# Experts' outputs stored by indirect DMA into two dense halves, and one later transfer that fills the empty slots of a mixture of experts

## The reference, cut to what matters

```python
def ffn(x, ...):                       # x: 1024 tokens x 256
    ys = geglu(xf @ Ws1 + bs1) @ Ws2 + bs2            # shared expert
    logits = (xf @ Wr + br) / TAU
    top_val, top_idx = top_k(logits, 2)               # two experts for each token
    top_w = softmax(top_val)
    h = einsum('nd,edh->enh', xf, We1) + be1          # 12 experts, 256 -> 2*768
    yE = einsum('enh,ehd->end', geglu(h), We2) + be2
    return ys + einsum('end,ne->nd', yE, w)           # w holds top_w at top_idx
```

## Time and profile before

| what | value |
|---|---|
| median of 3 runs | 1594.03 us (1591.66 to 1597.79) |
| the profiled execution | 1593.92 us, span 1592.2 us |
| TensorE busy | 1359.0 us, 85% |
| VectorE busy | 1344.2 us, 84% |
| ScalarE busy | 1053.1 us, 66% |
| GpSimd busy | 986.2 us, 62% |
| moved by DMA | 132.87 MB, mean 83 GB/s |
| queue of SP | 94696 packets, 62.99 MB |
| queue of GpSimd | 9312 packets, 67.90 MB |
| stages | start-up to 34, attention to 706, state space to about 1260, experts from 1279 to the end |

### The profile page before, as it was taken

The page is one execution under the profiler, slowest core; times in us unless marked ns, Lnnn a source line. Parts: engine busy times, 40 slices in busy tenths (PEclk is TensorE's granted clock), DMA queues, the critical chain, the costliest instruction groups (busy, mean ns, idle before and its releaser), DMA issues. The chain is left out here.

```text
span 1592.2 us, 33554 instructions
## 1 busy us (share of the span) xinstructions
PE 1359.0 (85%) x12662; PEld 1021.3 (64%) x12662; DVE 1344.2 (84%) x1703; ACT 1053.1 (66%) x2455; POOL 986.2 (62%) x828
## 2 busy tenths in 40 slices
PE   4899999999999999979677667677676899999992
PEld 4688888888888888765233333333333688888881
DVE  3899999999999999987599999999999635666662
ACT  3656666666666666535599899899899234555550
POOL 1778888788888878656166666666666341323323
PEclk9999999999999999999799999999999999999996
DMA  4511111111111111007454110200000016888872
GB/s 120 191 36 43 43 36 46 40 43 43 43 43 36 49 37 30 1 2 153 129 97 63 22 24 1 38 9 1 1 1 1 1 62 267 304 310 310 305 269 86
DMA packets 104155, 132.87 MB, mean 83 GB/s; under 512 B 39514, under 2 KB 95265, under 8 KB 100552
## 3 DMA queue, kind: packets, MB, share of 16 engines
q1 hardware_dynamic: 94696, 62.99, 16.1%
q0 software_dynamic: 9312, 67.90, 12.0%
HBM read 110.44 MB, written 14.45 MB: 78 GB/s over the span
## 5 line engine op out<-in xcount | busy, mean ns | idle before, releaser
L564 POOL TENSOR_TENSOR half<-prob 128x512 f32<-128x512 f32 (+1 forms) x208 | 266.7, 1282 | 108.5 <-ACT prob L600 106.9
L596 ACT ACTIVATE prob<-ps_s,mx 128x64 f32<-128x64 f32 (+1 forms) x624 | 151.5, 322 | 236.3 <-DVE prob L709 236.3
L1359 DVE TENSOR_TENSOR state<-ps_u,state 128x1024 f32<-128x1024 f32 x252 | 296.7, 1219 | 4.3
L704 DVE TENSOR_REDUCE mx<-ps_s 128x16 f32<-128x1024 f32 (+1 forms) x208 | 253.2, 1217 | 14.9 <-PE ps_s L637 11.2
L1318 PE MATMUL ps_y<-state,cz 128*32 128x256 f32 x2048 | 247.5, 384 | 2.1 <-DVE state L1359 1.1
L637 PE MATMUL ps_s<-qbd,kT 64*128 64x256 f32 (+1 forms) x1664 | 217.4, 396 | 23.0 <-ACT prob L596 17.5
L1245 ACT ACTIVATE ps_a<-A,dt 128x256 f32<-128x256 f32 x504 | 210.4, 463 | 35.1 <-DVE state L1354 35.1
L709 DVE TENSOR_TENSOR prob<-ps_s,mx 128x832 f32<-128x832 f32 (+1 forms) x208 | 213.0, 1024 | 7.1
L1229 POOL TENSOR_TENSOR state<-direct,state 128x1024 f32<-128x1024 f32 x64 | 151.6, 2369 | 84.3 <-PE ps_y L1318 84.2
L1300 PE MATMUL ps_u<-x_rows,b_diag 48*128 48x256 bf16 x1024 | 78.1, 272 | 138.2 <-DVE state L1359 134.8
L637 PEld LDWEIGHTS ps_s<-qbd,kT 64*128 64x128 f32 (+1 forms) x1664 | 151.0, 184 | 67.2 <-issue 35.9
(11 more groups left out here) (260 smaller groups left out, 3116.8 us busy)
## 6 DMA issues: line engine op xcount, KB each, us to landing
raw<-in_ctxT_dram SPq DMA_DIRECT2D x80, 268.0 KB, 2.8
x_rows<-ssm_x SPq DMA_DIRECT2D x96, 64.0 KB
raw<-in_ctxT_dram SPq DMA_DIRECT2D x16, 261.0 KB, 2.8
b_diag<-zeros SPq DMA_DIRECT2D x2, 2048.0 KB, 9.0
x_slots<-zeros SPq DMA_DIRECT2D x1, 3456.0 KB, 14.1
xg<-x_slots SPq DMA_DIRECT2D x27, 128.0 KB, 6.5
y_slots<-y SPq DMA_DIRECT2D x27, 128.0 KB, 4.5
ssm_x<-xp SPq DMA_DIRECT2D x6, 384.0 KB, 3.9
```

The costliest lines, as they stand in the source:

```text
L564: pool.tensor_tensor(half[0:rows, :, :], prob[0:rows, g % SLOTS, :, 0:L // 2], prob[0:rows, g % SLOTS, :, L // 2:L], ALU.add).then_inc(hal ...
L704: nc.vector.tensor_reduce(mx[0:rows, g % 2, :], part, AX_X, ALU.max, negate=True)\
L1359: nc.vector.tensor_tensor(h, flat(ps_u[k % 2][:, :, :]), h, ALU.add).then_inc(state_ready, 1)
```

## The change

Five edits belong together.

1. `x_slots` becomes `slot_rows`, a DRAM tensor whose rows have 257 elements: 256 features and a row number. A tile `blank` of 257 columns takes the place of `zeros`; its last column, `unused`, is made by an `iota` and holds 2048 plus the partition. One transfer fills all 3456 rows with it. It is issued behind the chunks of element 3 (CLEAR_AT), and the state-space loads behind those of element 5 (SSM_AT); both stood behind those of element 1.
2. At the head of `experts` GpSimd makes `rows`: for both choices the normalised tokens copied (128x2048 each) with the row number of the token (token, or 1024 + token) in the last column. The 16 scatters store rows of 257 elements.
3. In the routed loop SP no longer stores `y`. It loads for each tile the row numbers (`info`, one element a partition) two tiles ahead, once the put that used the buffer before has landed. GpSimd stores `y` with an indirect transfer (`put_rows`) at those row numbers of `routed`, which is the first 2176 rows of `y_slots`; unused slots go to the rows from 2048 on. The put of tile i-3 stands behind the weight loads of tile i.
4. VectorE's copy of `y` waits for the put that used the buffer, not for the store.
5. After the last put SP loads `back` with eight plain transfers, one for each token tile, of 256 rows each, in place of the 16 indirect gathers.

```diff
+        SSM_AT, CLEAR_AT = 5, 3
...
-                if n == 1:
+                if n == SSM_AT:
                     load_ssm(sp, d, m, ssm_loaded)
-                    sp.dma_start(d["x_slots"].rearrange("(t p) d -> p t d", p=P),
-                                 sb["zeros"][:, :].unsqueeze(1).broadcast_to([P, RTILES, D])).then_inc(slots_cleared, 16)
+                if n == CLEAR_AT:
+                    sp.wait_ge(ones_ready, 1)
+                    sp.dma_start(d["slot_rows"].rearrange("(t p) d -> p t d", p=P),
+                                 sb["blank"][:, :].unsqueeze(1).broadcast_to([P, RTILES, D + 1])).then_inc(slots_cleared, 16)
...
+            c.link(pool.iota(sb["unused"][:, :].bitcast(U32), pattern=[[0, 1]], base=2 * TOK, channel_multiplier=1,
+                             allow_small_or_imprecise_dtypes=True))
...
+            def load_info(T, turn, b):
+
+                if not known(turn, 1):
+                    sp.wait_ge(put[b], turn * 16)
+                with nc.allow_non_contiguous_dma(reason="one row number for each slot"):
+                    sp.dma_start(info[b][:, :], slot_rows(T)[:, D:D + 1]).then_inc(info_loaded[b], 16)
...
-                if not (isinstance(turn, int) and turn == RTILES // BUFS - 1):
+                ends = isinstance(turn, int) and turn == RTILES // BUFS - 1
+                if not ends:
                     load_x(T + BUFS, turn + 1, b)
-                sp.wait_ge(y_taken, T + 1)
-                sp.dma_start(d["y_slots"][bass.ds((T - TT) * P, P), :], y[b][:, :]).then_inc(y_stored[b], 16)
+                if not (ends and b):
+                    load_info(T + BUFS - 1, turn + 1 if b else turn, (b + BUFS - 1) % BUFS)
...
+            for b in range(BUFS):
+                sp.wait_ge(put[b], 16 * RTILES // BUFS)
+            for t in range(TT):
+                sp.dma_start(back[:, t, :, :], d["routed"][0:2 * TOK, :].rearrange("(i t p) d -> t p i d", i=2, p=P)[t])\
+                    .then_inc(y_back[t // 2], 16)
...
+            def put_rows(i):
+
+                b = i % BUFS
+                if i:
+                    pool.wait_ge(put[(i - 1) % BUFS], 16 * ((i - 1) // BUFS + 1))
+                pool.wait_ge(info_loaded[b], 16 * (i // BUFS + 1))
+                pool.wait_ge(y_taken, TT + i + 1)
+                pool.indirect_dma_start(d["routed"][:, :], bass.IndirectOffsetOnAxis(ap=info[b][:, :].bitcast(U32), axis=0),
+                                        y[b][:, :], None).then_inc(put[b], 16)
+
+            for i in range(2):
+                pool.iota(rows[:, :, i, D:D + 1].bitcast(U32), pattern=[[P, TT], [0, 1]], base=TOK * i,
+                          channel_multiplier=1, allow_small_or_imprecise_dtypes=True).then_inc(rows_made, 1)
+                pool.tensor_copy(rows[:, :, i, 0:D], f["xln"]).then_inc(rows_made, 1)
+            pool.wait_ge(rows_made, 4)
...
-                                            f["xln"][:, t, :], None).then_inc(scattered, 16)
+                                            rows[:, t, i, :], None).then_inc(scattered, 16)
...
-            for b in range(BUFS):
-                pool.wait_ge(y_stored[b], 16 * RTILES // BUFS)
-            for t in range(TT):
-                for i in range(2):
-                    j = 2 * t + i
-                    pool.indirect_dma_start(back[:, t, i, :], None, d["y_slots"][:, :],
-                                            bass.IndirectOffsetOnAxis(ap=slot[:, j:j + 1], axis=0))\
-                        .then_inc(y_back[t], 16)
+                if i >= BUFS:
+                    put_rows(i - BUFS)
+            for i in range(RTILES - BUFS, RTILES):
+                put_rows(i)
...
-                        dve.wait_ge(y_stored[b], turn * 16)
+                        dve.wait_ge(put[b], turn * 16)
...
-                    dve.wait_ge(y_back[t], 32)
+                    dve.wait_ge(y_back[t // 2], 32)
```

More of the change, by code:

```diff
@@ L669, in outputs @@
                 ins.then_inc(pv_done, 1)
-            pe.wait_ge(ones_ready, 4)
+            pe.wait_ge(ones_ready, 5)
             pe.wait_ge(bv_chain, 9)
@@ L1688, in experts @@
         x_loaded = [sem(f"e_x_loaded{b}") for b in range(BUFS)]
-        y_stored = [sem(f"e_y_stored{b}") for b in range(BUFS)]
-        y_back = [sem(f"e_y_back{t}") for t in range(TT)]
+        rows = sbuf("rows", [P, TT, 2, D + 1])
+        info = [sbuf(f"info_{b}", [P, 1]) for b in range(BUFS)]
+        info_loaded = [sem(f"e_info_loaded{b}") for b in range(BUFS)]
+        put = [sem(f"e_put{b}") for b in range(BUFS)]
+        rows_made = sem("e_rows_made")
+        y_back = [sem(f"e_y_back{p}") for p in range(TT // 2)]
         x_turned, xTh_ready, xT_ready = sem("e_x_turned"), sem("e_xTh_ready"), sem("e_xT_ready")
@@ L1746, in _, with slot_rows @@
         def _(sp):
+            def slot_rows(T):
+                return d["slot_rows"][bass.ds((T - TT) * P, P), :]
             def load_x(T, turn, b):
@@ L1750, in load_x @@
                     sp.wait_ge(x_turned, T - TT - BUFS + 1)
-                sp.dma_start(xg[b][:, :], d["x_slots"][bass.ds((T - TT) * P, P), :]).then_inc(x_loaded[b], 16)
+                sp.dma_start(xg[b][:, :], slot_rows(T)[:, 0:D]).then_inc(x_loaded[b], 16)
+            def load_info(T, turn, b):
[3 more added lines that the diff above has]
+                    sp.dma_start(info[b][:, :], slot_rows(T)[:, D:D + 1]).then_inc(info_loaded[b], 16)
             def one(kind, T, turn, b):
-                if not (isinstance(turn, int) and turn == RTILES // BUFS - 1):
+                ends = isinstance(turn, int) and turn == RTILES // BUFS - 1
+                if not ends:
                     load_x(T + BUFS, turn + 1, b)
-                sp.wait_ge(y_taken, T + 1)
-                sp.dma_start(d["y_slots"][bass.ds((T - TT) * P, P), :], y[b][:, :]).then_inc(y_stored[b], 16)
+                if not (ends and b):
+                    load_info(T + BUFS - 1, turn + 1 if b else turn, (b + BUFS - 1) % BUFS)
             sp.wait_ge(scattered, 16 * 2 * TT)
@@ L1761, in _ @@
                 load_x(TT + b, 0, b)
+            for b in range(BUFS - 1):
+                load_info(TT + b, 0, b)
             all_tiles(sp, one, routed_only=True)
+            for b in range(BUFS):
[3 more added lines that the diff above has]
+                    .then_inc(y_back[t // 2], 16)
             for t in range(TT):
@@ L1774, in _ @@
                     j = 2 * t + i
-                    pool.indirect_dma_start(d["x_slots"][:, :],
+                    pool.indirect_dma_start(d["slot_rows"][:, :],
                                             bass.IndirectOffsetOnAxis(ap=slot[:, j:j + 1], axis=0),
-                                            f["xln"][:, t, :], None).then_inc(scattered, 16)
+                                            rows[:, t, i, :], None).then_inc(scattered, 16)
             pool.wait_ge(owner_ready, 1)
@@ L2089, in perceiver_layer @@
               "gmask": sbuf("gmask", [P, HG]),
-              "minus_half": sbuf("minus_half", [P, TT]), "zeros": sbuf("zeros", [P, D])}
+              "minus_half": sbuf("minus_half", [P, TT]), "blank": sbuf("blank", [P, D + 1])}
+        sb["zeros"], sb["unused"] = sb["blank"][:, 0:D], sb["blank"][:, D:D + 1]
+        d["slot_rows"] = nc.dram_tensor("slot_rows", (RTILES * P, D + 1), F32, kind="Internal").ap()
+        d["routed"] = d["y_slots"][0:2 * TOK + P, :]
         slots_cleared = ctx.enter_context(nc.semaphore("slots_cleared"))
```

## The result

The changed kernel takes **1574.75 us** (median of 4 runs, 1574.38 to 1575.61); the kernel before, run beside it, 1594.89 us (1591.66 to 1597.79). The ratio is 0.9875, 95% interval 0.9855 to 0.9895. The forecast was 1579 us, range 1572 to 1588, faster with a chance of 0.86.

What follows compares the result with a forecast made beforehand. No single owner was seen (TensorE 85% busy, VectorE 84%), with TensorE bounding the routed tiles. Terms −8.4 + 3.0 + 0.5 − 10.3 = −15.2 us, from a median of 1594.03, gave 1579 us, range 1572 to 1588.

Steps and rivals of the forecast that it cites:

- the four terms: Head of attention −8.4 us, GpSimd's copies +3.0, routed stage +0.5, tail −10.3.
- rival 1: Head of the experts: GpSimd's copies don't hold VectorE up, `hid` comes in time, 1576 us; chance 0.22.
- the best tail: Tail: the favourable bound of its term, −11.5 us; with rival 1 it makes −19.9, 1574 us.
- The head of attention: Start of attention: moving the loads behind later chunks removes the stall, −8.4 us, bounds 4.8 and 8.4.
- rival 2: Head of attention: the stall moves instead of going, at worst paid at element 3, 1587 us; chance 0.12.
- GpSimd's copies: Head of the experts: two copies hold up VectorE's operations, so `hid` is late, +3.0 us, bounds 0 and 6.4.
- The routed stage: Routed loop: w1 is issued 1.25 us later, just above the slacks, +0.5 us, bounds 0 and 19.
- Rival 3: Routed loop: w1 late in every turn, turns grow by 0.8 us, 19 in all, 1597 us; chance 0.07.
- The tail: After the last `y`: one put and eight loads replace sixteen gathers, −10.3 us, bounds −6 and −11.5.
- Rival 4: Tail: eight loads wait for each other or the put, −6 instead of −10.3, 1583 us; chance 0.10.
- The closing: After the last sums: 4.6 us of output store and closing stay, change 0.

Runs made afterwards that it cites:

- m2: Changed kernel with state-space loads and clearing both back behind element 1: 1587.98 us, ratio 0.9963 to the kernel before.
- m4: Changed kernel with only the state-space loads back behind element 1: 1593.96 us, one run, on a chip where the changed kernel has 1592.0.
- m3: Changed kernel with only the clearing back behind element 1: 1581.33 us, one run.
- c1: Changed kernel with GpSimd's two copies of 128x2048 ahead of the scatters made twice: 1576.74 us, ratio 0.9896 to the kernel before.
- p2: Changed kernel with every put issued a second time, into rows nobody reads: 1600.91 us, ratio 0.9944 to the kernel before.
- p1: Changed kernel with each put issued after the first weight load of the next turn: 1601.79 us, ratio 0.9939 to the kernel before.
- d1: Changed kernel with one more indirect load on GpSimd after the seventh tile's sums: 1600.61 us, ratio 0.9937 to the kernel before.
- m1: Kernel before with only the state-space loads and clearing moved (elements 5 and 3), rows still 256 wide: 1588.28 us, ratio 0.9968 to the kernel before.
- p3: Changed kernel with the put as in p1 and SyncE loading each tile's row numbers one tile later: 1590.91 us, ratio 0.9869 to the kernel before.
- after_again: The changed kernel, unaltered, run again in the third set on another chip: 1592.0 us, ratio 0.9887 to the kernel before.

## Why the prediction was right, and where its terms were off

The sign, the range and three of the four terms held by their mechanisms. That the time lies only 2.75 us inside the range's lower end is partly luck: the range reached down there for rival 1, the best tail and the spread of runs, and not for the shorter closing, which no term or rival held.

*The head of attention*, −8.4 forecast, −7.0 in the two pairs (and 0.5 from the start-up, which no step of mine touches). The cause was read rightly: m2 brings the stall back, and m4 and m3 show that moving the clearing alone is enough and moving the loads alone nearly so, which the forecast left open. The size was off because the normal length of the two pairs was taken from the one after them, 6.3 us each, where they take 14.1: I subtracted 12.6. There was room at element 3, and rival 2 is out: no split waits at 3 or 5. The wide clearing came to 18.7 us in the trace after and to 15.8 to 18.7 in all, where the estimate by the Trainium skill ("DMA: Bandwidth & Descriptors", "How a descriptor splits into AXI transactions") was 17; the 256-wide clearing takes 12.8 to 14.1. The traces agree with the rule that rows off a 256-byte boundary cost more.

*GpSimd's copies*, +3.0 forecast, 0 measured: **this is the step that failed**. "3.7 us each, 7.4 both" was worked out from the copies of line 944, 1.71 ns for an element. The new copies took 1.88 us for 2048 elements, 0.92 ns each, half. The copies of line 944 reorder their rows by step and by token on both sides, and the new ones run straight along each row of `rows`; that this makes the difference is the likely reason, but no run varies it alone. The Trainium skill's "GPSIMD Engine Reference", section "Engine selection", says of GpSimd that "1-input is roughly line-rate". The straight copies agree: 0.92 ns an element is no slower than VectorE's own pace here (1.76 us for the 1536 elements of `w1l`, 1.15 ns each); the reordering ones do not. With the copies over before `pick`, only `diff` (+0.88) and `atf` (+0.63) were held up, 1.5 us in all, and `hid` still ended 1.19 us before it was needed. c1 gives the copies the length that I had assumed and gets a stall of 2.34 us, near the 3.0 forecast. It was rival 1's outcome, though not for its reason: the copies do hold VectorE up, for too short a time.

*The routed stage*, +0.5 forecast, +0.3 measured. Measured from the w2 before it, w1's issue starts 2.06 us later than before but ends only 1.34 later (1495.88 + 0.96 − 1492.58 = 4.26 against 1500.90 + 1.68 − 1499.66 = 2.92), since it is now the put that runs into VectorE's product (below) and w1 no longer is. That is close to the 1.25 forecast, and so is the landing: in the 16 turns between 1400 and 1540 us w1 lands 12.2 us after the start of the w2 before it, where it was 11.1 (medians). The median of 9.2 us that the forecast used mixes w1 and w2; w1 alone took 9.2 to 10.6, median 9.9, so it was nearer to its limit than I wrote, and the 7.3 after is such a mixture too. ScalarE's waits of up to 1.2 us (1.1 was forecast for the worst turn) come in 13 tiles and not in a few, and stay within the 1.36 us that I had counted behind ScalarE. Rival 3 is out: the turns did not grow, and even p2, with yet 1.3 us more in each turn, loses 3.0 us in the stage and not 19. What the forecast passed over in one sentence ("SP now waits for the put of a tile to land before it loads further `x`") is the tighter place: p1 shows it to cost 11.7 us as soon as the put starts some 2 us later in its turn.

*The tail*, −10.3 forecast, −10.0 measured, by the same steps: the put 0.79 us behind the copy instead of 0.3, landing 2.39 instead of 2.4, first sum 6.74 us behind the copy's end instead of 6.6, sums over 8.2 us instead of 8.1. Rival 4 is out.

*The closing*: "Only 4.6 us of output store and closing follow up to the span's end, and they stay". They did not; 2.5 of them went. I took the output store for the end of the span. It was GpSimd's drain, held by the gathers that the change takes away: it ended at 1591.98, 2.5 us after SyncE was done with the stores. d1 puts an indirect transfer back and brings 6.5 us, and m1, which keeps the gathers, keeps a closing of 4.5 us. The chain on the page does not tell the two cases apart (it names GpSimd's last line after the change too); the rows of the drain do.

Summed: −15.2 forecast, + 0.9 (head, with the start-up), − 2.9 (copies), − 0.2 (routed), + 0.3 (tail), − 2.5 (closing) = −19.6 by these rounded terms, 19.5 by the spans.

## What to carry to other kernels

A price per element may hold only for the access pattern it was measured with: before taking an engine's rate from another row, look in the code whether both walk memory in the same way. Ask of the last microseconds what ends them; here GpSimd closes 7 to 9 us after its last indirect transfer, so it should issue that one early. And where one queue does two jobs in turn, a wait added for one of them delays the other: let it wait for an event as old as the buffers allow, as p3 does.

## What the runs showed of the hardware

*An indirect issue that starts while VectorE subtracts two SBUF tensors (`w1l`) is held until that ends.* Before, 23 of GpSimd's weight issues in the routed stage took 1.68 to 1.80 us instead of 0.94; each began while VectorE's `w1l` (1.76 us) was running and ended 0.81 us after it. After, all 25 long ones are puts; the one below ends 0.88 us after. Two rows of after:

```profile
1492.93 1.76 DVE L2072 TENSOR_TENSOR w1l<-w,w1h 128x1536 fp32r<-128x1536 f32 x1
...
1493.82 1.75 POOL L1805 DMA_INDIRECT y_slots<-y,info  x1 [0.30 <-issue]
```

1492.93 + 1.76 = 1494.69, and the put ends at 1495.57. An issue that was under way when `w1l` began took its 0.94. The Trainium skill ("SBUF — State Buffer", "Who interferes with whom") infers that descriptor generation is not held by such an operation; the measurement says otherwise here.

*GpSimd's closing drain* ended 7.1 us after the end of its last indirect issue in the two kernels that close with gathers (before, m1), 8.0 in the ten that close with one put, 8.1 in d1 and 8.9 in p2, which closes with two puts.

*Two chips were 17 us slower*, with the kernel before as with all others. In the eight traces of changed kernels there (58.0 to 58.5 us) it lies in the shared tiles of the experts: from the first transposes of `hid` to those of `x` 58.1 us in after_again instead of 40.1, with waits that the profile puts down to "remote", and a mean granted clock of 0.63 in the first row below. Busy time by stretch and a row of ScalarE, after_again:

```profile
1295.00:1317.00 22.00, 10.19 (x31) 7.21 (x32) 1.10 (x3) 2.17 (x6) 9.79 (x11) 0.63 0.76 296
```

```profile
1310.02 0.38 ACT L1945 ACTIVATE gel<-e_ps_g 128x256 f32<-128x256 f32 x1 [13.71 <-remote]
```

In the traces before, after and of the first set the same stretch takes 39.7 to 40.1 us and shows no such wait. What it waits for is open; no run here tells it.
